# The bit stage of a chained eight-stage kernel on one core: gate bias as a sixth product on TensorE, scaling and rounding on ScalarE, the next block quantised inside the last tile, seven unused products before each output projection

## What is computed

```python
def bit_linear(x, w, b):
    gamma_x = jnp.clip(jnp.max(jnp.abs(x), axis=-1, keepdims=True), 1e-05, None)
    scale_x = 127.0 / gamma_x
    x_dq = jnp.clip(jnp.round(x * scale_x), -128.0, 127.0) / scale_x
    gamma_w = jnp.clip(jnp.mean(jnp.abs(w)), 1e-05, None)
    w_dq = jnp.clip(jnp.round(w / gamma_w), -1.0, 1.0) * gamma_w
    return jnp.einsum('bsd,hd->bsh', x_dq, w_dq) + b
```

## Time and profile before

| | |
|---|---|
| median of three executions | 1612.32 us |
| the profiled execution, its own time | 1609.94 us |
| its span, first to last instruction | 1608.1 us |
| TensorE busy | 1263.4 us (79%) |
| VectorE busy | 1009.5 us (63%) |
| ScalarE / GpSimd busy | 475.0 us / 329.5 us |
| mean granted TensorE clock | 0.914 of full speed |
| bit stage | from 919 us to 1085 us of the span |

### The profile page before, as it was taken

One profiled execution on the slowest core, in us unless ns is written; L12 is line 12 of the kernel. 1 busy time (PEld: TensorE's weight loads), 2 busy tenths in 40 slices (PEclk: granted clock), 3 DMA queues, 4 the chain that ended last, 5 costly groups with the idle time before them and its releaser, 6 DMA issues.

```text
span 1608.1 us, 19984 instructions
## 1 busy us (share of the span) xinstructions
PE 1263.4 (79%) x6665; PEld 715.0 (44%) x6670; DVE 1009.5 (63%) x2401; ACT 475.0 (30%) x664; POOL 329.5 (20%) x319
## 2 busy tenths in 40 slices
PE   0127999999979989957777545555898989999997
PEld 0114454545434456635555423222454545456554
DVE  8994353535255256558977789984888888822222
ACT  3462122222103133322222122220454545531110
POOL 2120000000023500023454243334343334000000
PEclk9999999999989999978988656675999999999999
DMA  9100000002000010011101000003232322100001
GB/s 322 30 13 1 0 0 0 0 0 108 1 20 0 14 52 0 1 26 27 26 0 27 3 18 0 0 1 88 88 91 76 90 75 90 41 1 0 0 0 52
DMA packets 67467, 55.68 MB, mean 35 GB/s; under 512 B 23888, under 2 KB 60624, under 8 KB 67152
## 3 DMA queue, kind: packets, MB, share of 16 engines
q1 hardware_dynamic: 66768, 54.67, 11.3%
q10 hardware_dynamic: 640, 0.26, 0.1%
HBM read 39.97 MB, written 14.68 MB: 34 GB/s over the span
## 4 chain that ended last, share of the span: by engine, by line
PE 64%; DVE 19%; issue 11%; ACT 3%; POOL 2%; DMA 1%; DVEq 1%; SPq 0%; POOLq 0%; ACTq 0%
PE banks L1021 7%; PE banks L2030 7%; PE banks L420 6%; PE banks L637 6%; PE banks L416 5%; PE banks L854 3%; PE banks L1028 3%; PE banks L846 3%; PE banks L427 3%; PE banks L431 3%; PE banks L1995 2%; DVE sb_work L1778 2%; DVE sb_work L2268 1%; PE banks L1346 1%; PE banks L1980 1%
## 5 line engine op out<-in xcount | busy, mean ns | idle before, releaser
L2268 DVE TENSOR_REDUCE sb_work<-banks 128x2 f32<-128x512 f32 x256 | 164.7, 685 | 47.0 <-PE banks L1995 44.8
L2139 ACT ACTIVATE sb_work<-banks 128x1024 f32<-128x1024 f32 x128 | 130.9, 1024 | 125.2 <-PE banks L2016 125.1
L537 DVE TENSOR_TENSOR sb_work<-sb_work,banks 128x512 f32<-128x512 f32 x72 | 49.4, 686 | 126.0 <-ACT sb_work L504 126.0
L1459 POOL TENSOR_TENSOR sb_work<-sb_work,sb_consts 128x512 f32<-128x512 f32 x64 | 68.6, 1104 | 247.2 <-ACT sb_work L1403 228.0
L1021 PE MATMUL banks<-sb_work,sb_shelf 128*128 128x512 f32 x256 | 114.4, 592 | 0.0
L420 PE MATMUL banks<-sb_work,sb_shelf 128*128 128x512 f32 (+1 forms) x192 | 92.2, 630 | 8.6 <-DVE sb_work L580 8.6
L997 POOL TENSOR_TENSOR sb_late<-sb_w2n 128x1024 f32<-128x1024 f32 x10 | 22.7, 2267 | 363.1 <-DVE sb_work L691 362.5
L504 ACT ACTIVATE sb_work<-banks 128x512 f32<-128x512 f32 x72 | 42.9, 596 | 181.6 <-PE banks L416 116.2
L637 PE MATMUL banks<-sb_work,sb_ctx_nat 128*64 128x512 f32 (+15 forms) x512 | 89.8, 509 | 7.8 <-DVE sb_work L699 7.8
L1100 DVE TENSOR_TENSOR sb_work<-sb_work,banks 128x512 f32<-128x512 f32 x32 | 22.0, 688 | 112.8 <-ACT sb_work L1086 112.8
L416 PE MATMUL banks<-sb_work,sb_shelf 128*128 128x512 f32 (+1 forms) x192 | 84.9, 593 | 0.0
(11 more groups left out here) (285 smaller groups left out, 2491.6 us busy)
## 6 DMA issues: line engine op xcount, KB each, us to landing
sb_work<-scratch SPq DMA_DIRECT2D x64, 192.0 KB
scratch<-sb_work SPq DMA_DIRECT2D x32, 192.0 KB, 2.1
sb_work<-ctx_t SPq DMA_DIRECT2D x16, 256.0 KB, 4.2
scratch<-sb_work SPq DMA_DIRECT2D x32, 128.0 KB, 2.1
sb_work<-ctx_t SPq DMA_DIRECT2D x4, 512.0 KB, 3.6
sb_ctx_nat<-ctx SPq DMA_DIRECT2D x1, 2048.0 KB, 10.8
sb_raw<-wguT SPq DMA_DIRECT2D x1, 2048.0 KB, 15.2
scratch<-sb_work SPq DMA_DIRECT2D x32, 64.0 KB, 1.8
```

Source lines behind the costliest of these rows:

```text
L1459: ins = nc.gpsimd.tensor_tensor(km_[:, hf, k, :, :], keys.unsqueeze(1).broadcast_to([P, 8, SEQ]), hm2.unsqueeze(2).broadcast_to([P, 8, SEQ ...
L2139: nc.scalar.activation(pt3[:, h % 2, :, :], o, ACT.Exp).then_inc(exp3, 1)
L2268: nc.vector.tensor_reduce(out=mx3[:, tc, k, 2 * hp:2 * hp + 2], in_=bank[u % 2].rearrange("p (h s) -> p h s", h=2), axis=AX, op=ALU.max).t ...
```

## The change

- **Gate bias on TensorE.** The gate bias, divided by the weight scale, is split into three bf16 parts, which lie in six rows of one tile (`b_rows`). The inverse token scale (`qr`) is split into three bf16 parts as well, and TensorE turns it into six rows (`r_rows`). One more product of K = 6 per half then adds bias divided by scales to the gate's sums.
- **Scaling on ScalarE.** Silu reads the bank itself and multiplies by the token's factor; VectorE keeps only the value's pass. The first rounding pass over the products (L1793) becomes a ScalarE activation (`rounded`) between `measure` and a shorter `to_ints`.
- **Order.** `ints` and `turn` of the next block go into the last tile (t = 3) of a block; `gate_value` of its tile 0 precedes `out_proj(2)`; `finish(3)` moves behind `value` of the next block's tile 1. The normalisation is split over tiles 1 and 2. The token factors are made inside `quantise`.
- **Seven unused products** (`keep_running`) stand before each output projection. They write to a bank that has been read.
- **Rows of ones by transfer.** The memset of `kS` goes; two transfers from `groups` write its rows of ones. `attn3_consts` moves behind the first split of the inverse scales, and waits for `b_int_ready`.
- Small: three semaphores of the weight scales become one (`gam_step`), three of attn2 become one (`w2_step`), `groups_ready` becomes `consts_ready`; six small transfers (`bit_rows`) write `b_rows`, on SyncE's queue behind `attn2_sync`; VectorE's block 0 is written out before the loop.

```diff
 def bit_rows(sp):
+    sp.wait_ge(b_split, 1)
+    for j, (_, piece) in enumerate(SPLITS2):
+        sp.dma_start(b_rows[j:j + 1, :], b_parts[:, piece, :]).then_inc(bit_b_in, 16)
...
 def bit_prep_vector(dve, link):
...
+    dve.wait_ge(bit_b_in, 48)
+    link(nc.vector.tensor_scalar(b_flat, b_flat, gamr[:, 0:1], None, ALU.mult))
+    for piece in range(3):
+        ins = nc.vector.tensor_copy(b_parts[:, piece, :], b_flat)
+        if piece < 2:
+            link(ins)
+            link(nc.vector.tensor_tensor(b_flat, b_flat, b_parts[:, piece, :], ALU.subtract))
...
 def gate_value(b, t, f, before=None):
...
+    if n == 0:
+        pe.wait_ge(b_intT_ready, 2 * b + 2)
+    nc.tensor.matmul(bank[2 * (n % 3)], r_rows[:, t * P:(t + 1) * P],
+                     b_rows[:, f * 512:(f + 1) * 512], start=False, stop=True).then_inc(b_gv, 1)
...
 def turn(b):
...
+    pe.wait_ge(r_parts_ready, b + 1)
+    pe.wait_ge(b_intT_ready, 2 * b + 1)
+    for t in range(BT):
+        ins = nc.tensor.transpose(bf_bank(6)[0:len(SPLITS2), t * P:(t + 1) * P], r_parts[:, t, :], ident_h[:, :])
+    ins.then_inc(b_turned, 1)
+
+def keep_running(b, t):
+    i, n = (0, 3) if t == 0 else (4, 5)
+    for done in (b_silu, bv_ready):
+        pe.wait_ge(done, 8 * b + n + 1)
+    for _ in range(7):
+        nc.tensor.matmul(bank[i], ident_h[:, :], gwT[:, 0, 0, 0:512], start=True, stop=True)
...
 TensorE block_
+                    elif not last:
+                        turn(b + 1)
+                        for f in range(2):
+                            gate_value(b + 1, 0, f, before=b)
                     out_proj(b, t - 1)
-                if not last:
-                    turn(b + 1)
-                    pe.wait_ge(b_intT_ready, b + 2)
-                    for f in range(2):
-                        gate_value(b + 1, 0, f, before=b)
                 out_proj(b, BT - 1)
...
 ScalarE block_
                 for t in range(1, BT):
                     silu(b, t)
+                    rounded(b, t - 1)
+                    if t == BT - 1 and not last:
+                        ints(b + 1)
                     turned(b, t - 1)
                 if not last:
-                    ints(b + 1)
+                    silu(b + 1, 0, before=b)
+                rounded(b, BT - 1)
                 turned(b, BT - 1)
-                if not last:
-                    silu(b + 1, 0)
...
 GpSimd
+            inverse_parts(0)
+            attn3_consts(pool, link, ph + 1)
             pool.wait_ge(ob_ready, 1)
+            with pool.Fori(0, BLOCKS - 1) as b:
+                products(b)
+                inverse_parts(b + 1)
...
 VectorE ints
+                    dve.wait_ge(b_turned, 2 * b)
+                    dve.wait_ge(b_silu, 8 * b)
 VectorE block_
                 for t in range(1, BT):
-                    gate_value(b, t)
+                    value(b, t)
+                    if t == 1 and (not isinstance(b, int) or b > 0):
+                        finish(b - 1, BT - 1)
+                    measure(b, t - 1)
+                    if t == 1:
+                        for step in range(2):
+                            normalise(link, (b + 1) % BLOCKS, step=step)
+                    elif t == 2:
+                        normalise(link, (b + 1) % BLOCKS, step=2)
+                    elif not last:
+                        ints(b + 1)
                     to_ints(b, t - 1)
                     if t > 1:
                         finish(b, t - 2)
-                    if t == 1:
-                        normalise(link, (b + 1) % BLOCKS)
-                if not last:
-                    ints(b + 1)
+                measure(b, BT - 1)
                 to_ints(b, BT - 1)
                 finish(b, BT - 2)
                 if not last:
-                    gate_value(b + 1, 0, before=b)
-                finish(b, BT - 1)
+                    value(b + 1, 0, before=b)
...
 attn3
+                sp.dma_start(kS[rows.stop - 2:rows.stop, :, :, :].rearrange("p i h (n c) -> p (i h n) c", c=SEQ),
+                             groups[0:2, 0:SEQ].unsqueeze(1).broadcast_to([2, BT * H3 * C3 // SEQ, SEQ])).then_inc(a3_in, 16)
...
-            nc.gpsimd.memset(kS, 1.0).then_inc(vv_clear, 1)
```

More of the change, by code:

```diff
@@ L1125, in quantise @@
             link(nc.vector.reciprocal(qr[:, :], qs[:, :]))
+            if scales is not None:
+                for k in range(2):
+                    nc.vector.tensor_scalar(scales[:, k, :], qs[:, :], gam[:, k:k + 1], None, ALU.mult)
             for t in range(BT):
@@ L1245, in attn2_prep_vector @@
             link(ins)
-            nc.vector.tensor_scalar(w_int, w_nat, -ROUND, 127.0, ALU.add, ALU.min).then_inc(w2_int, 1)
+            nc.vector.tensor_scalar(w_int, w_nat, -ROUND, 127.0, ALU.add, ALU.min).then_inc(w2_step, 1)
             for par in range(2):
@@ L1622, in flamingo_kernel @@
         bv, at = part(work, at, [P, 2, 512])
+        r_rest, at = part(work, at, [P, BT])
+        r_parts, at = part(work, at, [P, BT, len(SPLITS2)], BF16)
+        r_rows, at = part(work, at, [len(SPLITS2), BTOK], BF16)
         bh, at = part(work, at, [P, 2, FF2])
@@ L1745, in bit_gpsimd, with inverse_parts, products @@
         def bit_gpsimd(pool, link, ph):
-            pool.wait_ge(ob_ready, 1)
-            with pool.Fori(0, BLOCKS) as b:
+            def inverse_parts(b):
+                pool.wait_ge(b_int_ready, b + 1)
+                one = ones[:, 0:1].unsqueeze(2)
+                link(nc.gpsimd.tensor_tensor(r_parts[:, :, 0:3], qr[:, :].unsqueeze(2).broadcast_to([P, BT, 3]),
+                                             one.broadcast_to([P, BT, 3]), ALU.mult))
+                link(nc.gpsimd.tensor_tensor(r_rest, qr[:, :], r_parts[:, :, 0], ALU.subtract))
+                link(nc.gpsimd.tensor_tensor(r_parts[:, :, 3:5], r_rest.unsqueeze(2).broadcast_to([P, BT, 2]),
+                                             one.broadcast_to([P, BT, 2]), ALU.mult))
+                nc.gpsimd.tensor_tensor(r_parts[:, :, 5], r_rest, r_parts[:, :, 3], ALU.subtract).then_inc(r_parts_ready, 1)
+            def products(b):
                 for t in range(BT):
@@ L1767, in bit_vector, with value @@
             link(nc.vector.tensor_scalar(gam[:, 2:3], gam[:, 2:3], gates[:, 6:7], None, ALU.mult))
-            def gate_value(b, t, before=None):
+            def value(b, t, before=None):
                 for f in range(2):
@@ L1776, in gate_value, with measure @@
                     dve.wait_ge(b_gv, 8 * b + n + 1)
-                    for k, (dst, done) in enumerate(((bg, bg_ready), (bv, bv_ready))):
-                        nc.vector.scalar_tensor_tensor(
-                            out=dst[:, f, :], in0=bank[2 * (n % 3) + k], scalar=tok_scale[:, k, t:t + 1],
-                            in1=gb_b[:, k, f * 512:(f + 1) * 512], op0=ALU.mult, op1=ALU.add).then_inc(done, 1)
-            def to_ints(b, t):
+                    nc.vector.scalar_tensor_tensor(
+                        out=bv[:, f, :], in0=bank[2 * (n % 3) + 1], scalar=tok_scale[:, 1, t:t + 1],
+                        in1=vb_b[:, f * 512:(f + 1) * 512], op0=ALU.mult, op1=ALU.add).then_inc(bv_ready, 1)
+            def measure(b, t):
                 dve.wait_ge(bh_ready, 8 * b + 2 * t + 2)
@@ L1923, in attn3_sync @@
             for k in range(2):
+                rows = stack_rows(k, MROW + 2)
+                sp.dma_start(kS[rows.stop - 2:rows.stop, :, :, :].rearrange("p i h (n c) -> p (i h n) c", c=SEQ),
+                             groups[0:2, 0:SEQ].unsqueeze(1).broadcast_to([2, BT * H3 * C3 // SEQ, SEQ])).then_inc(a3_in, 16)
+            for k in range(2):
                 sp.dma_start(b3[k * SEQ:(k + 1) * SEQ, :], a["b3"]).then_inc(a3_in, 16)
@@ L2377, in _ @@
             attn2_sync(sp, PHASE["attn2"])
+            bit_rows(sp)
             sp.wait_ge(bit_w_ready, 3)
@@ L2428, in _ @@
             attn2_gpsimd(pool, link, PHASE["attn2"])
-            attn3_consts(pool, link, PHASE["attn3"])
             bit_gpsimd(pool, link, PHASE["bit"])
```

131 lines of the change are left out of this document (79 added, 52 removed).

## The result

The changed kernel took 1636.14 us (median of four, 1633.6 to 1638.79), the kernel before beside it 1612.68: a ratio of 1.0143, 95% interval 1.0127 to 1.0159. It is 23.5 us slower, where I forecast 5.7 us slower (1618.0) and a range up to 1627. The sign was right, the time lies outside the range. Two single executions far above all others (one of the kernel before at 1733.75 us, one of `round_dve` at 2634.09 us) are left out of every ratio.

A forecast was written before the change was run, and what follows sets the result against it. VectorE bounds the stage before; afterwards a chain across TensorE and ScalarE: 146 + 0.37 x 58 = 167.5 us, less 7.0 for the earlier start, against 154.4, so 6 us slower: 1618 us, range 1601 to 1627.

The forecast's parts named there:

- The start of the stage: First quantisation of the bit stage: without the memset of `kS` beside it, whole numbers ready 7.0 us earlier, at 923.3.
- The new wait for ScalarE's rounding behind `turned(2)`: Block's end: `rounded(3)` queued behind `turned(2)`; 3.2 us on the chain, VectorE waiting 5 us or more.
- The clock: TensorE in the bit stage: two falls per block, 0.37 at the low level, granted clock 0.82 where it was 0.66.
- The relief of VectorE is spent on the chain across TensorE and ScalarE: Middle blocks: 38 us less VectorE work in the stage, yet 37.1 us a block at full clock against 38.9 and 37.0.
- The first rival (clock pays): Bit stage: unused products carry the clock; low level 0.15 gives 7 us faster, none 15 us faster (1597); chance 0.22.
- Frame: Whole kernel: the difference within the profiled execution is added to the median of 1612.32, giving 1618.
- The stage itself: Four blocks of the bit stage: 167.5 us, less the earlier start of 7.0, against 154.4 before.
- my two sums of each: Each block at full and half clock: first 29 and 38, middle ones 37 and 52, last 43 and 62 us.
- the bias product: TensorE's added product per half: counted as one more product of 512 columns, 0.216 us at full clock.
- my own 58: Bit stage: 146 us all at full clock, 204 all at half; the low-level share 0.37 multiplies these 58 us.
- GpSimd's inverse part: Four GpSimd instructions in quantisation: 0 to 5 us, taken 0.9; at the upper end 3 us more a block.
- The port: VectorE's fast passes beside GpSimd's products on the shared port pair: taken as 0, at most 1.05 a block, 4 us.

The follow-up runs named there:

- round_dve: Changed kernel without unused products, with 50 padding memsets, the rounding put back from ScalarE on VectorE: ratio 1.0039 to the kernel before, blocks 168.5 us.
- no_bias: Changed kernel without unused products, with padding, without the 6-row gate-bias product (gate bias left out of the output): ratio 0.9998 to the kernel before, blocks 160.5 us.
- nb_rdve: Changed kernel without unused products and without the gate-bias product, with padding, rounding back on VectorE: ratio 0.9957 to the kernel before, blocks 154.6 us.

## Why the prediction was wrong

**Right.** The start of the stage: 7.0 forecast; 7.2 by the start leg, 6.4 with the transfers alone. The new wait for ScalarE's rounding behind `turned(2)`, its place and that it is long. The clock: 0.82 forecast, 0.79. The relief of VectorE is spent on the chain across TensorE and ScalarE: shown by the runs, in which taking work off TensorE (no_bias) or the hop to ScalarE away (round_dve) shortens the blocks while VectorE's work stays or grows. The first rival (clock pays) is refuted twice, in the changed kernel and in the kernel before. The sign is no luck: without the stall the changed kernel still has 1.0103.

**What failed.** The sum had two holes of about equal size in the profile. The stage is the one that carries the time out of the range: without the stall, 1.0103 times 1612.3 is 1629, still over 1627, while 1618 and the stall's 5 to 9 us would have stayed within it.

- *No term for the stages behind.* "Frame" added a difference within the bit stage to the median, as if the rest were fixed. It took 8.9 us more in the profile, 7.1 of them at and behind the stall of 4.67 us; by the ratios the stall is worth 5.3 to 6.5 us. The front said that VectorE's block 0 is written out before the loop; the prediction costed it nowhere. Nothing in the trace of before showed a stall of this kind, so it could not be priced, but it belonged in the range.
- *The stage itself*: 167.5 forecast, 176.7 by the same bounds, 9 us. All four blocks are over: by 3.3, 2.6, 1.1 and 2.2 us when my two sums of each are mixed by the forecast's own low-clock share of 0.37. The term shown to be mis-sized is **the bias product**, taken as one more of 0.216. It comes to 0.60 and a gap of 0.84 at half clock: four products and the bias take 2.35 us (961.13 to 963.48), I had 2.13; at full clock 1.29, I had 1.08. At full clock that is the price of two products. Over 128 rows, where it has the price of one as in my sum, the blocks are 7.2 us shorter. The clock is next: 0.79 is 0.42 at the low level instead of 0.37, 3 us by my own 58. The rounding took 1.25, not 1.06. The six-row copy was right (0.59, taken 0.6), and so was GpSimd's inverse part: 1.44 us in the second block (958.49 to 959.93), done before TensorE turned it at 960.61. The range should have held its upper end of 3 us a block, and did not. The port, taken 0 with 4 as the most, shows on L156, some 1.5 us a block longer (2.79 to 2.97 against 1.38), 6 us of VectorE's time in all. Added up, these terms are more than 9 us, so not all of them are on the path.

**The rival of the clock.** I priced the clock at 58 us between its two levels, and the unused products at 1.5 on the chain at each block's end. They cost 5.7 and 8.7 us, all gains of clock included. A clock that rises because of work on the chain is paid for by that work.

**The port** may be the cause of L156's length, by the earlier trace rows and the Trainium skill's rule that the prediction quoted: in every block L156 starts 0.4 to 0.6 us after two GpSimd products of 2.54 us together (945.03 after 944.61). No run here moved L156 by itself, so that stays argued, and so does its price: in `nb_rdve` it still takes 2.90 to 2.91 us, and the blocks are as short as before. Why the rounding's undoing gives 3.3, 5.9 or 7.1 us by what else is undone was not traced to single waits either.

## What to carry to other kernels

Before moving work off the busiest engine, undo one moved part at a time on the new order and read the stretch, not the longest wait: here the longest wait (9.0 us a block at most) was worth 2.7 us in all, and 32 products that looked like 0.2 us each were worth 11.3. Compare stages that the edit doesn't touch as well, since a program that gets longer can move a loop elsewhere into a stall; if one appears, some tens of instructions of padding tell. Ask of fillers for the clock what stands behind them: in both kernels here the next turn did, and they cost more than the clock gave back. A place where they pay was not tried.

## What was not expected of the hardware

- A TensorE product with 6 rows between products with 128 rows costs more than one with 128: the weight load isn't brought forward (gap 0.84 us at half clock and 0.42 at full, instead of 0.28 and none), nor is the next one's. The Trainium skill (TensorE: Matmul & The Clock Gate, "Step-by-step: what each phase is for") says that a load's time doesn't depend on the rows, and that loads are pulled ahead when the row groups don't conflict or the load goes to the background weight buffer. As for the first, the load itself is no longer with 6 rows (0.093 us in the mean, 0.11 with 128); here the pull-ahead is what is lost, and the measurement decides. Why it is lost no run shows.
- The position of a loop of 300 VectorE instructions, shifted by 28 (74 memsets ahead of it instead of 46), costs 4.8 us of stall, and 5 to 6.5 us of the total.
